# Two layers of one Trainium2 kernel in one program block: each wait of the second layer on its producer, in place of the drain and the barrier

## The reference

```python
x = _layernorm(x + _L0_attn_ref(x, ...))   # 4-head retention with rotary, rms norm, silu gate
x = _layernorm(x + _L0_ffn_ref(x, ...))    # 8 experts, top 2, F = 256
x = _layernorm(x + _L1_attn_ref(x, ...))   # 8-head retention (dense decay mask), group norm, silu gate
x = _layernorm(x + _L1_ffn_ref(x, ...))    # 8 experts, top 2, F = 512
```

## Time and profile before

| what | value |
| --- | --- |
| time, median of 3 runs | 1265.44 us (1263.67 to 1267.41) |
| profiled execution: span, first to last instruction | 1352.5 us, 31553 instructions |
| profiled execution: a time of its own beside the span | none is given |
| mean granted TensorE clock | 0.929 |
| PE busy | 1160.4 us (86%) |
| DVE, ACT, POOL busy | 904.9 (67%), 739.8 (55%), 741.5 (55%) us |
| DMA | 101.78 MB, mean 75 GB/s |

### The profile page before, as it was taken

One profiled execution on the slowest core, in us unless ns is written; L12 is line 12 of the kernel. 1 busy time (PEld: TensorE's weight loads), 2 busy tenths in 40 slices (PEclk: granted clock), 3 DMA queues, 4 the chain that ended last, 5 costly groups with the idle time before them and its releaser, 6 DMA issues.

```text
span 1352.5 us, 31553 instructions
## 1 busy us (share of the span) xinstructions
PE 1160.4 (86%) x10358; PEld 1029.9 (76%) x10358; DVE 904.9 (67%) x2658; ACT 739.8 (55%) x2016; POOL 741.5 (55%) x901
## 2 busy tenths in 40 slices
PE   6999999985477888884899999986689999999992
PEld 5888888874376888873577676665679999999992
DVE  4788888867345655552688887886557666666883
ACT  2343444532344655553466677774446666666884
POOL 0266677755464666655016666656644444444675
PEclk9999999985788999886899999998689999999996
DMA  8212112011124222222223112101121121112553
GB/s 236 65 51 58 48 45 71 31 32 48 32 86 113 80 86 81 83 88 101 84 79 96 58 60 62 45 30 50 48 82 57 56 57 57 56 57 78 171 173 121
DMA packets 75424, 101.78 MB, mean 75 GB/s; under 512 B 15138, under 2 KB 51490, under 8 KB 74850
## 3 DMA queue, kind: packets, MB, share of 16 engines
q1 hardware_dynamic: 49538, 59.89, 15.7%
q0 software_dynamic: 17280, 35.69, 7.9%
q10 hardware_dynamic: 8448, 4.20, 1.0%
HBM read 59.87 MB, written 43.04 MB: 76 GB/s over the span
## 4 chain that ended last, share of the span: by engine, by line
PE 32%; DVE 7%; ACT 5%; issue 4%; POOL 2%; another core or an unknown queue 2%; DMA 1%; ACTq 0%; DVEq 0%; SPq 0%; POOLq 0%
PE banks L2208 14%; PE banks L2227 9%; DVE b_sT L1982 2%; PE banks L2136 1%; PE banks L2192 1%; DMA scattered<-b_r_x,b_r_idx 1%; ACT b_cn_sq L283 1%; PE banks L2303 1%; PE banks L2302 1%; ACT b_n_sq L283 1%; PE banks L2153 1%; ACT b_qx L1906 1%; PE banks L2239 0%; PE banks L2264 0%
## 5 line engine op out<-in xcount | busy, mean ns | idle before, releaser
L1733 POOL DMA_INDIRECT expert_out<-e_ysb,b_e_idx x142 | 162.8, 1147 | 161.2 <-ACT e_ysb L1839 133.9
L869 POOL DMA_INDIRECT expert_out<-a_e_ysb,a_e_idx x142 | 151.3, 1065 | 93.9 <-ACT a_e_ysb L922 52.8
L2208 PE MATMUL banks<-b_e_x_hi,e_w_hi 128*128 128x256 f32 x568 | 168.5, 297 | 5.9 <-ACT e_sgl L1829 2.4
L2208 PE MATMUL banks<-b_e_x_hi,e_w_lo 128*128 128x256 f32 x568 | 162.0, 285 | 1.4 <-issue 1.4
L472 POOL DMA_INDIRECT scattered<-a_r_x,a_r_idx x128 | 128.9, 1007 | 36.0 <-issue 36.0
L2227 PE MATMUL banks<-w_dn,e_h 128*128 x1136 | 140.0, 277 | 1.9 <-DVE e_h L2028 0.8
L2227 PEld LDWEIGHTS banks<-w_dn,e_h 128*128 128x128 f32 x1136 | 134.2, 194 | 2.7 <-issue 2.6
L2028 DVE TENSOR_TENSOR e_h<-banks,e_sgl 128x512 f32<-128x512 f32 x142 | 97.2, 689 | 55.2 <-PE banks L2208 44.7
L472 POOL DMA_INDIRECT scattered<-b_r_x,b_r_idx x112 | 111.3, 993 | 31.0 <-issue 30.7
L1829 ACT ACTIVATE e_sgl<-banks 128x512 f32<-128x512 f32 x142 | 85.1, 600 | 75.8 <-DVE e_h L2028 39.1
L2016 DVE TENSOR_TENSOR e_w_lo<-w_gu,e_w_hi 128x1024 fp32r<-128x1024 f32 x71 | 87.2, 1228 | 54.9 <-ACT e_w_hi L1818 44.5
(11 more groups left out here) (375 smaller groups left out, 3319.4 us busy)
## 6 DMA issues: line engine op xcount, KB each, us to landing
a_e_xg<-scattered SPq DMA_DIRECT2D x71, 130.0 KB
b_e_xg<-scattered SPq DMA_DIRECT2D x71, 130.0 KB
b_cy<-expert_out SPq DMA_DIRECT2D x32, 256.0 KB
f_y<-expert_out SPq DMA_DIRECT2D x32, 256.0 KB
a_xT<-in_x_T SPq DMA_DIRECT2D x16, 256.0 KB
out<-f_x ACTq DMA_DIRECT2D x16, 256.0 KB
expert_out<-a_e_ysb,a_e_idx POOLq DMA_INDIRECT x142
expert_out<-e_ysb,b_e_idx POOLq DMA_INDIRECT x142
```

What stands on the lines that cost most here:

```text
L869: nc.gpsimd.indirect_dma_start(out=expert_out, out_offset=bass.IndirectOffsetOnAxis(ap=idx[n % 4][:, i:i + 1], axis=0), in_=ysb[n % 4][:, ...
L1733: nc.gpsimd.indirect_dma_start(out=expert_out, out_offset=bass.IndirectOffsetOnAxis(ap=idx[n % 4][:, i:i + 1], axis=0), in_=ysb[n % 4][:, ...
L2208: mm = nc.tensor.matmul(bank_of(c, j)[:, i * ROWS:(i + 1) * ROWS], w_[c % RING][:, g, f:f + P], x_[c % RING][:], start=(m == 0), stop=(m = ...
```

## The change

The two blocks and the block between them become one. What is done to the waits:

- The first layer's semaphores fall into two kinds. Those of its attention are cleared by POOL in mid-stream, after the scatters of tile 48, and a small instruction then signals `s_cleared`. Those of its experts (`late_sem`) keep their numbers to the end and are never cleared.
- POOL no longer waits for the landing of its scatters at the layer's end, only for `e_y_mm` = 71 (PE has finished the last tile, so the layer's buffers may be overwritten).
- In the second layer every engine waits for `s_cleared`; PE also for the last `e_ysb` copy and for the folded weights. SP waits for `e_y_mm` = 71 before it overwrites an expert's weights, and for the landing of all scatters only before sequence 11 (`EARLY`) is loaded, since the earlier ones lie in tiles that have long landed.
- ACT no longer loads its function table at the start of layer 2.
- The buffers `e_xg` of layer 2 move to another place in SBUF.

```diff
-        def clear_semaphores():
-            with nc.Block() as between:
-                @between.gpsimd
-                def _(pool):
-                    numbers = sorted(s.num for s in used)
...
-                        pool.sem_clear(range(numbers[at], numbers[to] + 1))
-                        at = to + 1
-            used.clear()
+        def clear_finished():
+            numbers = sorted(s.num for s in used)
...
+                nc.gpsimd.sem_clear(range(numbers[at], numbers[to] + 1))
+                at = to + 1
@@ first_layer
+                def late_sem(name):
+                    return whole.enter_context(nc.semaphore("a_" + name))
-                block = ph.enter_context(nc.Block())
+                CLEARING = 48
@@ first_layer, POOL
-                    for i in range(2):
-                        pool.wait_ge(router.sent[i], SCATTERS * SEQS // 2)
-                    for i in range(4):
-                        pool.wait_ge(e_st[i], SENT * ((STEPS + 3 - i) // 4))
+                        if n == CLEARING:
+                            clear_finished()
+                            wait_apart(pool, 4).then_inc(s_cleared, 1)
+                    pool.wait_ge(e_y_mm, STEPS)
@@ second_layer, SP
+                    sp.wait_ge(s_cleared, 1)
                     for s in range(AHEAD, SEQS):
                         z = turns(s)[0]
+                        if z.n == EARLY:
+                            for i in range(4):
+                                sp.wait_ge(st_sems[0][i], SENT * ((STEPS + 3 - i) // 4))
                         comb.load(sp, z)
+                        if z.n == 2:
+                            sp.wait_ge(first.y_mm, STEPS)
                         if 2 <= z.n < 2 + E:
                             load_expert(sp, 1, z.n - 2, s_wx1)
@@ second_layer, ACT
-                    nc.scalar.preload_act_table_set("silu_and_others")
+                    act.wait_ge(s_cleared, 1)
@@ second_layer, DVE
+                    dve.wait_ge(s_cleared, 1)
@@ second_layer, PE
+                    pe.wait_ge(s_cleared, 1)
+                    pe.wait_ge(first.y_there, STEPS)
+                    pe.wait_ge(first.wv_there, 1)
+                    pe.wait_ge(first.w2_there, 2)
+                    pe.wait_ge(first.set_there, 2)
@@
-            first_layer()
-            clear_semaphores()
-            second_layer()
+            with nc.Block() as block:
+                second_layer(block, first_layer(block))
```

More of the change, by code:

```diff
@@ L145, in build @@
         s_early = whole.enter_context(nc.semaphore("s_early"))
+        s_cleared = whole.enter_context(nc.semaphore("s_cleared"))
         def load_expert(sp, layer, e, sem):
@@ L161, in new_sem @@
             return used[-1]
-        def clear_semaphores():
-            with nc.Block() as between:
-                @between.gpsimd
-                def _(pool):
-                    numbers = sorted(s.num for s in used)
[L168 to L172, removed]
-                        pool.sem_clear(range(numbers[at], numbers[to] + 1))
-                        at = to + 1
-            used.clear()
+        def clear_finished():
+            numbers = sorted(s.num for s in used)
+            at = 0
+            while at < len(numbers):
+                to = at
+                while to + 1 < len(numbers) and numbers[to + 1] == numbers[to] + 1:
+                    to += 1
+                nc.gpsimd.sem_clear(range(numbers[at], numbers[to] + 1))
+                at = to + 1
         mark = keep("mark", [1, 13])
@@ L614, in second_rows, with first_layer @@
                 nc.vector.tensor_scalar(t_row[:, k], rowf, self.first2[0:1, 0:1], None, ALU.add).then_inc(self.there, 1)
-        def first_layer():
+        def first_layer(block):
             ph = ExitStack()
@@ L668, in first_layer @@
                 x1 = router.x[0]
-                tables = SplitTables(sb, over, sem, "w_raw", "qm")
+                tables = SplitTables(sb, over, late_sem, "w_raw", "qm")
                 FC, RING = F0 // P, 4
@@ L714, in first_layer @@
                 SENT = 16 * (ROWS // P)
-                e_ld = [sem(f"e_ld{i}") for i in range(4)]
+                e_ld = [late_sem(f"e_ld{i}") for i in range(4)]
                 e_st = st_sems[0]
[L717 to L721, removed]
+                e_x_mm, e_x_hi_there, e_x_ev = late_sem("e_x_mm"), late_sem("e_x_hi_there"), late_sem("e_x_ev")
+                e_w_hi_there, e_w_there = late_sem("e_w_hi_there"), late_sem("e_w_there")
+                e_g_mm, e_u_mm, e_sg_there, e_h_there = late_sem("e_g_mm"), late_sem("e_u_mm"), late_sem("e_sg_there"), late_sem("e_h_there")
+                e_y_mm, e_y_there = late_sem("e_y_mm"), late_sem("e_y_there")
+                e_at_there, e_idx_there = late_sem("e_at_there"), late_sem("e_idx_there")
                 e_summed, e_centered = sem("e_summed"), sem("e_centered")
                 s_lx, s_ex, s_dif, s_th = sem("lx"), sem("ex_there"), sem("dif"), sem("th")
-                wv_mm, wv_there = sem("wv_mm"), sem("wv_there")
-                w2_mm, w2_there = sem("w2_mm"), sem("w2_there")
-                gb_mm, gb_hi_there, set_there = sem("gb_mm"), sem("gb_hi_there"), sem("set_there")
+                wv_mm, wv_there = late_sem("wv_mm"), late_sem("wv_there")
+                w2_mm, w2_there = late_sem("w2_mm"), late_sem("w2_there")
+                gb_mm, gb_hi_there, set_there = late_sem("gb_mm"), late_sem("gb_hi_there"), late_sem("set_there")
                 w_vT, c_center, w_2T, c_mean, g_w, g_b = early[2], early[3], early[5], early[6], early[7], early[8]
@@ L1469, in _ @@
                             nc.tensor.matmul(G_BANK[0:1, 0:D], g_b[:], w_2[:], start=True, stop=True).then_inc(gb_mm, 1)
+            return Ends(e_y_mm, e_y_there, wv_there, w2_there, set_there)
         class Combine:
@@ L1533, in sum_second, with __init__, second_layer @@
                 dve.wait_ge(self.used, t.n + 1)
-        def second_layer():
+        class Ends:
+            def __init__(self, y_mm, y_there, wv_there, w2_there, set_there):
+                self.y_mm, self.y_there = y_mm, y_there
+                self.wv_there, self.w2_there, self.set_there = wv_there, w2_there, set_there
+        def second_layer(block, first):
             ph = ExitStack()
@@ L1554, in second_layer @@
                 w_q, w_k, w_vT, c_center, w_1, w_2T, c_mean, g_w, g_b, t_q, t_k, m_head, m_par, m_blk, w_r = early
+                xg = [sb(f"e_xg{i}", [P, ROWS // P, WIDE]) for i in range(4)]
                 xT = [sb(f"xT{i}", [P, T]) for i in range(2)]
@@ L1588, in second_layer @@
                 idx = [sb(f"e_idx{i}", [P, ROWS // P], U32) for i in range(4)]
-                xg = [sb(f"e_xg{i}", [P, ROWS // P, WIDE]) for i in range(4)]
                 x_hi = [sb(f"e_x_hi{i}", [P, ROWS], F32R) for i in range(RING)]
```

## The result

| | before | after |
| --- | --- | --- |
| time, median of 6 runs | 1264.0 us (1262.84 to 1267.41) | 1253.11 us (1251.48 to 1258.67) |
| ratio after / before | | 0.9908, 95% interval 0.9889 to 0.9928 |
| profiled execution: span | 1352.5 us | 1256.9 us (its own time 1258.67) |
| mean granted TensorE clock | 0.929 | 0.947 |

Faster by 10.9 us between the medians, where 11.0 was forecast (1254.4, from a median of 1265.44). The ratio says 11.6 us, with an interval of 9.1 to 14.0, so an agreement to 0.1 us is partly luck. The span, though, fell by 95.6 us, far more than the time. So the two spans of the table must not be subtracted. What can be compared is a distance inside the seam.

The account below looks back on a forecast made before the run. The prediction took the barrier seam between the layers as on the path, with POOL's scatter queue deciding once it goes. 11.8 - 0.5 = 11.3 us, taken as 11.0 in timed runs, gave 1254.4 us; range 1249 to 1260.5.

Parts of the forecast that it names:

- PE's restart: Layer 2's first matmul: starts near 620.7 instead of 634.15, behind the last `e_ysb` copy and folded weights, 13.5 us earlier.
- The memset of `b_vz`: POOL, layer 2's start: memsets queue behind the last scatters, ACT's first value copy waits for them; gain 11.8 us, not 13.5.
- Does POOL take the memset at once?: Behind POOL's last scatter: memset starts with 0 us delay, 2.85 us as bound if the drain is POOL's own work.
- The clock, 0.5 us: PE's first scores, behind a new 2 us idle time: half clock may cost 0 to 2.3 us, taken as 0.5.
- The clearing, 0 under a cover of 3.12 us: POOL after tile 48: clearing and small instruction take 1.8 us, hidden by 3.12 us of idle time behind tile 50: 0.
- SP's loads: Sequence 3 and two experts' weights, issued at about 617.6 beside POOL's last scatters: 0 us, bound 1.7.
- DVE beside the scatters: Layer 2's start: DVE instructions reading PSUM don't lengthen POOL's scatters: 0 us, bound 1.0.
- From the profile to the timed runs: Whole kernel: 11.3 us in the profile, scaled by 0.936 to 10.6; 11.0 taken between the two.
- POOL isn't what binds: Rival at the seam: scatters quicker unprofiled or backlog shorter, PE's restart decides; 1249 to 1253 us, chance 0.13.
- shorter seam: Rival: seam shorter than profiled, or POOL's drain is real work that stays; 1256.5 to 1260.5 us, chance 0.20.
- given back: Rival: something later in layer 2 is tied to a moment, so no change; 1265 us, chance 0.05.
- slower: Rival: without the pause PE passes the front of layer 2 at 1.2 GHz for longer; 1269 us, chance 0.04.

Follow-up runs that it names:

- experiment 2: The kernel after, with PE's first matmul of layer 2 made to wait for POOL's two memsets: 1261.26 us, ratio 0.9969.
- experiment 3: The kernel after, with the two memsets of `b_vz` moved from POOL to DVE: 1250.33 us, ratio 0.9883.
- experiment 5: The kernel after, with POOL's wait for the landing of all scatters put back ahead of its memsets: 1258.33 us, ratio 0.9933.
- experiment 8: The kernel of experiment 3, with sequence 1's norm on ACT moved behind the last `e_ysb` copies: 1248.5 us, ratio 0.9877.
- experiment 1: The kernel before, unchanged, run again for a second profile: 1265.8 us, ratio 1.0012, span 1261.4 us.
- experiment 6: The kernel after, with ACT's function table load put back ahead of layer 2: 1253.21 us, ratio 0.9915.
- experiment 7: The kernel after, with SP's first expert weights and sequence 3's rows held until POOL's memsets are done: 1251.29 us, ratio 0.9896.
- experiment 4: The kernel before, barriers kept, with POOL's wait for its last scatters' landing moved to SP ahead of sequence 11: 1263.34 us, ratio 0.9985.

## Why the prediction was right

- **The seam is on the path; what ends last is the question.** Right. The chain of the kernel after goes through POOL's scatters and memsets, and experiments 2, 3 and 5 move the first value copy by moving one wait each, with times that go the same way.
- **PE's restart.** Right in mechanism: 0.2 us behind the last `e_ysb` copy. The idle time was 1.94 us, 1.6 forecast. The full clock that it might have kept did not hold in this execution (0.56 in the first window); only experiment 8, with 1.63 us of idle time, held it throughout, and the second sequence gave back 1.4 of the 1.5 us that this gained.
- **The memset of `b_vz`, 11.8 us and not 13.5.** Right to a tenth: the copy was forecast 1.5 us behind the last scatter and came 1.46 behind. Experiment 3 takes the wait away and gets 2.2 us.
- **Does POOL take the memset at once?** Yes, in four kernels out of four that have it behind the scatters without a wait. The drain's 2.85 us is not work that a following instruction would meet. It isn't the price of every drain either: the next one on POOL, behind the clearing, took 0.03 us:

```profile
L164 POOLq DRAIN  x1: 34/34/34, 633.7 to 633.7; - x1
```

  The bound of 2.85 us, which made the range's upper end, was not used.
- **The clock, 0.5 us.** The mechanism was right, its size twice that in this execution. The first two value copies stood 14.00 us apart in the kernel after; where the clock held between them it was 12.94 (experiments 1 and 3), 12.95 (6), 12.96 (7) and 12.97 (4). All of the 1.05 us lies between the first scores and the second, 4.66 us in the kernel after and 3.61 in experiment 1. The prediction counted two groups of scores as exposed; it was one group and, more than that, the state matmuls behind it (`L2164`, 2.73 us against 1.61). In experiments 6 and 7 PE waited 1.94 and 2.87 us in the same place and the clock held, so a wait of this length may cost a microsecond or nothing; the runs don't show what decides. In the first profile of before the distance was 14.30, and in experiments 2 and 8 it was 14.36, with the clock full through the scores: there it fell later, behind PE's wait of 1.90 us for DVE's masks (0.50 from 570 to 572 in experiment 2). The prediction had read that fall, but not that it comes and goes from one execution to the next.
- **The clearing, 0 under a cover of 3.12 us.** The 0 was right, its ground was not. None of the nine profiles taken after the first, that of the kernel after included, has such an idle stretch ahead of a scatter of `L869`: it belonged to the drawn-out layer 1 of the first profile alone. The three clearings took 0.47 us together, not 1.65, and POOL's sequencer did them ahead of time, at 488.2 to 488.6, while a scatter of 1.44 us from 487.94 on kept POOL busy:

```profile
L172 POOLq EVENT_SEMAPHORE_RANGE_CLEAR  x3: 67/137/262, 488.2 to 488.6; - x3
```

  What is left in POOL's stream is the small instruction that signals `s_cleared`:

```profile
495.43 0.97 POOL L869 DMA_INDIRECT expert_out<-a_e_ysb,a_e_idx  x1 [0.30 <-issue]
496.42 0.18 POOL L181 TENSOR_TENSOR mark<-c_half 1x1 f32<-1x1 f32 x1
496.76 0.99 POOL L869 DMA_INDIRECT expert_out<-a_e_ysb,a_e_idx  x1 [0.16 <-issue]
```

  From the scatter's start to the next it is 1.33 us where 1.27 is the rule, so 0.06 us and not 1.8.
- **SP's loads, the table load, DVE beside the scatters: 0.** Right, by experiments 7 and 6, and by the six scatters behind PE's restart, 0.96 us each in the kernel after. Two DVE instructions that read PSUM ran beside the scatter at 554.38 (from 554.10 and from 554.71), and it too took 0.96. The one pair of rows from which this was forecast holds for the whole stage: in the two profiles of before and the one of after, all 77 scatters of `L869` over 1.15 us overlapped DVE's `a_e_w_lo` instruction, which has both inputs in SBUF, and none of the 202 that didn't overlap it was over 1.15 us. Of the scatters that did overlap it, 147 stayed under 1.15 us, so it lengthens some and not all.
- **From the profile to the timed runs, 11.3 us to 11.0.** The seam doesn't scale with the span: the same 13 us stand in executions of 1352.5 and 1261.4 us. The factor 0.936 should have been 1 for it. The two slips, 0.3 us too little here and 0.5 too much in the clock, nearly cancel; that is luck.
- **The rivals.** "POOL isn't what binds" fell, and so did "shorter seam", "given back" and "slower". The clock did fall behind the new wait, but it cost one microsecond and no stretch of several steps. A stretch of 8 us at half clock did appear in experiment 3, far behind the seam, and cost 4.8 us of that execution. From the first value copy to the end it is 702.8 us there, against 698.8 in the kernel after. What set it off isn't shown.

## What to carry to other kernels

A barrier between two stages costs what lies behind it twice: the machinery itself, here 3.8 us of landing, drain, clearing and signals, and the overlap it forbids, here the larger part, 7.85 us of first work that fitted under another engine's backlog. When it goes, look for the slowest queue at the seam and for any small set-up instruction in that queue; the next wait stands there. Giving that instruction to an idle engine took the wait away here (2.2 us in the trace). Measure such a step by a distance between two events at the seam in two profiles, never by the difference of spans.

## What was not expected of the hardware

- A drain on POOL behind indirect DMAs took 2.85 us when its scatters had already landed, and ended 2.9 us behind the last scatter when nothing had waited for them ahead of it (experiment 4), while a memset in the same place started within 0.01 us. POOL's next drain, with no scatter issued in between, took 0.03 us. On SP the drain of the same block took 0.13 us.
- A clearing of a range of semaphores took 0.55 us between two barriers. Three of them in a stream of scatters took 0.07 to 0.26 us each, beneath a scatter that was running.
- Idle times of PE of 1.94 and 2.87 us left the clock at 1.00 in one place of the program, and one of 1.91 us in the same place was followed by 0.50.
- One program's profiled executions differed by 91 us in span (1352.5 and 1261.4 us), 79 of them ahead of the seam.
